# The end of the last feed-forward: when GpSimd leaves, where the squares are summed, and how residual and store are cut

## The chip, the core and the metric

The kernel runs on one core of one Trainium2 chip. A core has TensorE (matrix products, PE in the profile), VectorE (DVE), ScalarE (ACT), GpSimd (POOL) and SyncE (SP), which here only issues DMAs. They run side by side and meet through semaphores. The metric is the device time of one execution in microseconds, the median of several runs; lower is better.

## The reference

Eight stages, each added to the running x of 1024 tokens (16 x 64) by 256 columns: four times an attention-like stage and a feed-forward, each behind a layernorm and a tanh gate. The change concerns the end of the last one.

```python
def _L3_ffn_ref(x, w_gate_up, w_proj):
    ...
    def rms_norm(x):
        eps = jnp.finfo(x.dtype).eps.astype(jnp.float32)
        xf = x.astype(jnp.float32)
        inv = jax.lax.rsqrt(jnp.mean(xf * xf, axis=-1, keepdims=True) + eps)
        return (xf * inv).astype(x.dtype)
    wq_gu = ternary_quant(w_gate_up)
    gu = jnp.einsum('bsd,hd->bsh', x, wq_gu)
    gate, up = jnp.split(gu, 2, axis=-1)
    h = jax.nn.silu(gate) * up
    hn = rms_norm(h)
    wq_p = ternary_quant(w_proj)
    return jnp.einsum('bsh,dh->bsd', hn, wq_p)
...
x = x + jnp.tanh(g_ffn[3]) * _L3_ffn_ref(_layernorm(x, axis=-1), L3_ffn_w_gate_up, L3_ffn_w_proj)
return x
```

h has 1024 columns. The rms norm divides a token's whole row by one number, so the kernel makes the down product from h as it is and multiplies the result by the token's scale.

## The kernel before

The program is written out by hand, engine by engine: one function for each stage and engine, and each engine runs its eight functions in a row (`PE_S`, `ACT_S`, `DVE_S`, `POOL_S`, and `SYNC` for the DMAs). Nothing schedules; the order on an engine is that of the code, and semaphores alone order the engines. x lies in SBUF all along as `xt` (`x_tok` in the profile), eight tiles of 128 tokens by 256 columns.

The last stage is f3. A step n of 16 takes one chunk of 128 of the 1024 hidden columns (`c`) and one half of the tokens (`half`, four tiles of 128). Four steps make a turn, the first turn is written out, the other three are a loop (`f3_loop`). In a step TensorE makes gate and up (line 3490), ScalarE the silu (3512), VectorE the product h (3540) and its square (3542). Since the products are bf16, h and its square are each split in a high and a low part: ScalarE makes `f3hh` and `f3qh` (3516, 3517), VectorE `f3ql` (3529, semaphore `f3_sl`), GpSimd `f3hl` (3567, `f_h_lo` in the profile, semaphore `f3_hl`). `down`, two steps behind, sums the squares over the chunk with a product against ones (3472, one column for each tile, into bank 6 of PSUM) and makes the down product (3475, 256 columns for each tile, into banks 0 to 3), tile by tile, squares and down product of one tile together; it counts up `f3_d`. The last two steps, 14 and 15, have their `down` behind the loop.

When all 16 are counted, VectorE makes the mean square of the eight tiles' tokens (3549), a reciprocal root of it by an integer seed and three Newton rounds (`rsqrt`, lines 161 to 166), the gate's factor (3551), and then for each tile the scaled down product plus x (3553). Through `dve_step` each of the small instructions waits for the one ahead of it.

Every f3 function ends in `finish(e, 9)`: it adds one to `stage_done` (line 146) and waits until the four engines have done so. SyncE waits for the same count, issues one DMA of all of x (3588), and waits for it to land. Behind the functions each engine comes to the end of the block (all recorded at line 84): it drains, reports to GpSimd, and is released by GpSimd when all have reported.

Of the kernel before, what the change touches and what calls it, by code (L numbers as in the profile page):

```python
# [21 lines left out]
ALU = mybir.AluOpType  # L22
# [3 lines left out]
P = 128  # L26
B, S, D = 16, 64, 256
N = B * S
NT = N // P
# [51 lines left out]
def program(nc, a):  # L81

    ctx = ExitStack()
    with ctx:
# [3 lines left out]
        def sem(name):  # L88
            return ctx.enter_context(nc.semaphore(name))


        xt = sb("x_tok", [P, NT, D])
# [8 lines left out]
        onesb = sb("ones_bf16", [P, 2], BF16)  # L101
# [17 lines left out]
        ps = ctx.enter_context(nc.psum_tensor("psum", [P, 8, 512], F32))  # L119
# [3 lines left out]
        dve_step, act_step, pool_step = Chain(sem("dve_step")), Chain(sem("act_step")), Chain(sem("pool_step"))  # L123
# [10 lines left out]
        x_stored = sem("x_stored")  # L134
# [5 lines left out]
        def done(eng, last=None):  # L140

            if last is not None:
                last.then_inc(pe_end, 1)
                n_pe_end[0] += 1
                eng.wait_ge(pe_end, n_pe_end[0])
            eng.sem_inc(stage_done, 1)

        def finish(eng, k, last=None):

            done(eng, last)  # L150
            eng.wait_ge(stage_done, 4 * k)
# [944 lines left out]
        c1_vr = sem("c1_values_ready")  # L1096
        c1_hl = sem("c1_qk_parts_ready")
# [6 lines left out]
        c1_x = sem("c1_x_ready")  # L1104
# [444 lines left out]
        FI = 1024  # L1549
# [1874 lines left out]
        F3_STEPS = 4  # L3424
        F3_TURNS = 2 * FI // P // F3_STEPS
# [3 lines left out]
        f3P = f3TP[:, 4 * FI:6 * FI].rearrange("p (c d) -> p c d", d=D)  # L3429
# [15 lines left out]
        f3_sf = sem("f3_squares_ready")  # L3445
        f3_sl = sem("f3_squares_lo_ready")
        f3_d = sem("f3_down_done")

        def f3_loop(e, body):

# [8 lines left out]
        def f3_pe(e):  # L3459

            turn_pe(e, 4, yt, 8)
            wait_yT(e, 4)
            e.wait_ge(*f3_in.at(64))

            def down(n, c, half, b, first):
                e.wait_ge(f3_hl, n + 1)
                e.wait_ge(f3_sl, n + 1)
                for j in range(4):
                    i = 4 * half + j
                    t = slice(j * P, (j + 1) * P)  # L3470
                    for x, l in enumerate((f3qh, f3ql)):
                        e.matmul(ps[:, 6, i:i + 1], l[:, b, t], onesb[:, 0:1], start=(first and i == 0 and x == 0), stop=False,
                                 skip_group_check=True)
                    for x, l in enumerate((f3hh, f3hl)):
                        ins = e.matmul(ps[:, i // 2, (i % 2) * D:(i % 2 + 1) * D], l[:, b, t], f3P[:, c, :],
                                       start=(first and i % 2 == 0 and x == 0), stop=False, skip_group_check=True)
                ins.then_inc(f3_d, 1)

            def body(it):
                fresh = isinstance(it, int)  # L3480
                for n_ in range(F3_STEPS):
                    n, half = F3_STEPS * it + n_, n_ % 2
                    tk = slice(half * HALF, (half + 1) * HALF)
                    for r, bank, done, ahead, filled in ((0, (4, 7)[n_ % 2], f3_si, 1, f3_g), (1, 5, f3_h, 0, f3_u)):
                        if not fresh or n_ > ahead:
                            e.wait_ge(done, n - ahead)
                        for kc in range(KC):
                            w = f3T[:, r, kc, bass.ds((2 * it + n_ // 2) * P, P)]
                            for x, y in enumerate((yTh, yTl)):
                                ins = e.matmul(ps[:, bank, :], w, y[:, kc, tk], start=(kc == 0 and x == 0), stop=(kc == KC - 1 and x == 1))  # L3490
                        ins.then_inc(filled, 1)
                    if not fresh or n_ > 1:
                        m_ = (n_ - 2) % F3_STEPS
                        c = 2 * it + n_ // 2 - 1
                        down(n - 2, c if fresh else bass.ds(c, 1), half, m_, fresh and n_ < 4)
            f3_loop(e, body)
            for n_ in (2, 3):
                down(F3_STEPS * (F3_TURNS - 1) + n_, FI // P - 1, n_ % 2, n_, False)
            e.wait_ge(f3_d, F3_STEPS * F3_TURNS)
            finish(e, 9)  # L3500

        def f3_act(e):
            turn_act(e, 4, yTh)

            def body(it):
                fresh = isinstance(it, int)
                for n_ in range(F3_STEPS):
                    n = F3_STEPS * it + n_
                    e.wait_ge(f3_g, n + 1)
                    if not fresh:  # L3510
                        e.wait_ge(f3_h, n - F3_STEPS + 1)
                    e.activation(f3g[:, n_, :], ps[:, (4, 7)[n_ % 2], :], ACT.Silu).then_inc(f3_si, 1)
                    e.wait_ge(f3_h, n + 1)
                    if not fresh:
                        e.wait_ge(f3_d, n - F3_STEPS + 1)
                    e.activation(f3hh[:, n_, :], f3h[:, n_, :], ACT.Copy).then_inc(f3_hh, 1)
                    e.activation(f3qh[:, n_, :], f3h[:, n_, :], ACT.Square).then_inc(f3_hh, 1)
            f3_loop(e, body)
            e.wait_ge(f3_hh, 2 * F3_STEPS * F3_TURNS)
            finish(e, 9)  # L3520

        def f3_dve(e):
            ln_tiles(e, NT - 1, NT)
            turn_dve(e, 4, yTh, yTl)

            def squares_lo(n, b):
                e.wait_ge(f3_hh, 2 * n + 2)
                e.wait_ge(f3_sf, n + 1)
                e.tensor_tensor(f3ql[:, b, :], f3sf[:, b % 2, :], f3qh[:, b, :], ALU.subtract).then_inc(f3_sl, 1)

            def body(it):
                fresh = isinstance(it, int)
                for n_ in range(F3_STEPS):
                    n = F3_STEPS * it + n_
                    e.wait_ge(f3_si, n + 1)
                    e.wait_ge(f3_u, n + 1)
                    if not fresh:
                        e.wait_ge(f3_hl, n - F3_STEPS + 1)
                        e.wait_ge(f3_hh, 2 * (n - F3_STEPS) + 2)
                    e.tensor_tensor(f3h[:, n_, :], ps[:, 5, :], f3g[:, n_, :], ALU.mult).then_inc(f3_h, 1)  # L3540
                    e.wait_ge(f3_h, n + 1)
                    e.tensor_tensor(f3sf[:, n_ % 2, :], f3h[:, n_, :], f3h[:, n_, :], ALU.mult).then_inc(f3_sf, 1)
                    if not fresh or n_ > 0:
                        squares_lo(n - 1, (n_ - 1) % F3_STEPS)
            f3_loop(e, body)
            squares_lo(F3_STEPS * F3_TURNS - 1, F3_STEPS - 1)
            e.wait_ge(f3_d, F3_STEPS * F3_TURNS)

            dve_step(e, e.tensor_scalar(f3v[:, :], ps[:, 6, 0:NT], 1.0 / FI, float(np.finfo(np.float32).eps), ALU.mult, ALU.add))
            rsqrt(e, dve_step, f3r[:, :], f3v[:, :], [NT])  # L3550
            dve_step(e, e.tensor_scalar(f3r[:, :], f3r[:, :], gates[:, 7:8], None, ALU.mult))
            for i in range(NT):
                ins = e.scalar_tensor_tensor(xt[:, i, :], ps[:, i // 2, (i % 2) * D:(i % 2 + 1) * D], f3r[:, i:i + 1], xt[:, i, :],
                                             ALU.mult, ALU.add)
            dve_step(e, ins)
            finish(e, 9)

        def f3_pool(e):
            def body(it):
                fresh = isinstance(it, int)  # L3560
                for n_ in range(F3_STEPS):
                    n = F3_STEPS * it + n_
                    e.wait_ge(f3_hh, 2 * n + 1)
                    if not fresh:
                        e.wait_ge(f3_d, n - F3_STEPS + 1)
                    e.wait_ge(f3_hh, 2 * n + 2)
                    e.tensor_tensor(f3hl[:, n_, :], f3h[:, n_, :], f3hh[:, n_, :], ALU.subtract).then_inc(f3_hl, 1)
            f3_loop(e, body)
            e.wait_ge(f3_hl, F3_STEPS * F3_TURNS)
            finish(e, 9)  # L3570


        SYNC = [l0_sync, c1_sync, m1_weights, lambda e: m1_sync(e, a2_ahead, a2_keys_values_ahead), a2_sync, lambda e: m2_sync(e, a3_ahead), a3_sync, f3_sync]
# [8 lines left out]
        @block.sync  # L3582
        def _(e):
            setup_sync(e)
            for stage in SYNC:
                stage(e)
            e.wait_ge(stage_done, 4 * (1 + len(PE_S)))
            e.dma_start(a["out"].rearrange("(t p) d -> p t d", p=P), xt[:, :, :]).then_inc(x_stored, 16)
            e.wait_ge(x_stored, 16)

        @block.tensor
        def _(e):
# [173 lines left out]
```

## Time and profile before

| | |
|---|---|
| median of 3 runs | 1300.43 us (1300.22 to 1301.52) |
| the profiled execution | 1304.3 us |
| its span, first to last instruction | 1302.5 us |
| VectorE's mean square of the last stage starts | 1287.07 us |
| its last residual ends | 1292.98 us |
| store issued, landing | 1293.06 us, 4.4 us later |
| last instruction | 1302.5 us |

Times inside the profile count from the span's start. In a row of the timeline the first number is the start and the second the time taken, both in us; the bracket at the end is the idle time ahead of it and what ended that. In a row by source line come the shortest, median and longest duration in ns, and the first and last start in us. A letter q behind an engine (POOLq) means its sequencer, which handles waits, branches and drains. The three runs and the profiled execution are different executions; the profiled one is 3.9 us longer than the median.

### The profile page before, as it was taken

How to read it: one execution, taken by the hardware profiler on the slowest of the kernel's cores; microseconds unless marked ns; L12 is line 12 of the kernel's file. 1: busy time of each engine (PE TensorE's matmuls, PEld its weight loads, DVE VectorE, ACT ScalarE, POOL GpSimd, SP SyncE). 2: the span in 40 equal slices, each digit the busy share in tenths (PEclk: the TensorE clock that was granted, in tenths of full speed). 3: DMA queues.
4: the chain of work that ended last, by engine and by line, in shares of the span. 5: the costliest groups of instructions: out<-in, count | busy, mean ns of one | idle time of the engine just before them, and what ended most of it. 6: DMA issues, size and time to landing. Idle time of an engine off the chain costs nothing.

```text
span 1302.5 us, 22884 instructions
## 1 busy us (share of the span) xinstructions
PE 1147.4 (88%) x8124; PEld 844.3 (65%) x8147; DVE 850.5 (65%) x1920; ACT 621.5 (48%) x1407; POOL 352.9 (27%) x328
## 2 busy tenths in 40 slices
PE   4867869999969999899999988888998999999894
PEld 3554644444455665889988746666657888898753
DVE  7788966888867663455546585333497777775664
ACT  5575435677733343344433422222266766666252
POOL 0040011222121002222222146566422433334032
PEclk8756976999969999899999889899999999999998
DMA  7010034000032235000000262522371000000100
GB/s 257 2 44 1 1 137 203 1 2 2 2 134 91 88 140 174 1 2 1 1 1 1 92 288 84 196 85 86 101 289 66 17 18 17 17 9 9 49 1 33
DMA packets 44571, 89.30 MB, mean 69 GB/s; under 512 B 7280, under 2 KB 30448, under 8 KB 42672
## 3 DMA queue, kind: packets, MB, share of 16 engines
q1 hardware_dynamic: 39184, 73.45, 15.7%
q0 software_dynamic: 5280, 14.42, 3.4%
q8 instruction: 67, 1.10, 0.4%
q14 instruction: 40, 0.33, 0.1%
HBM read 68.72 MB, written 21.10 MB: 69 GB/s over the span
## 4 chain that ended last, share of the span: by engine, by line
PE 65%; DVE 18%; issue 6%; ACT 5%; DMA 2%; POOL 2%; SPq 1%; another core or an unknown queue 1%; DVEq 0%; ACTq 0%; POOLq 0%; PEldq 0%
PE psum L2566 5%; PE psum L2154 4%; PE psum L3183 4%; PE psum L2126 4%; PE psum L3155 3%; PE psum L2586 3%; PE psum L1702 2%; PE psum L1274 2%; PE psum L3056 2%; PE psum L3103 2%; PE psum L2079 2%; PE psum L3125 2%; PE psum L3490 2%; PE psum L2057 2%; PE psum L1720 2%
## 5 line engine op out<-in xcount | busy, mean ns | idle before, releaser
L1469 DVE TENSOR_REDUCE c_max<-psum 128x2 f32<-128x512 f32 x128 | 84.2, 680 | 19.7 <-PE psum L1274 18.2
L1369 ACT ACTIVATE c_probs<-psum 128x512 f32<-128x512 f32 x128 | 75.1, 597 | 35.6 <-PE psum L1285 35.4
L2566 PE MATMUL psum<-m_experts,m_tileT 128*128 x188 | 69.2, 493 | 19.2 <-issue 13.4
L3183 PE MATMUL psum<-a_wo,a_outT 128*128 128x256 f32 x256 | 75.1, 405 | 0.7 <-DVE x_tok L3365 0.7
L2208 ACT ACTIVATE a_probs<-a_probs,a_max 128x64 f32<-128x64 f32 x128 | 42.7, 334 | 44.9 <-DVE a_max L2264 44.9
L3263 ACT ACTIVATE a_probs<-psum,a_max,a_q_rstd 128x128 f32<-128x128 f32 x128 | 56.8, 458 | 11.3 <-DVE a_max L3313 11.2
L2566 PEld LDWEIGHTS psum<-m_experts,m_tileT 128*128 128x128 f32 x188 | 35.8, 199 | 38.6 <-issue 27.9
L2126 PE MATMUL psum<-ctxT_yT_hi,a_wq 128*128 128x128 f32 x256 | 52.9, 290 | 8.2 <-DVE a_qT L2250 7.1
L2875 POOL DMA_INDIRECT m_back<-m_out_tiles,m_rows_of_slots x47 | 46.8, 995 | 46.9 <-DVE m_out_tiles L2809 39.6
L2643 ACT ACTIVATE m_tile_silu<-psum 128x176 f32<-128x176 f32 x47 | 14.9, 318 | 91.0 <-PE psum L2566 56.3
L2250 DVE TENSOR_TENSOR a_qT<-psum,a_columns 128x512 f32<-128x512 f32 x32 | 22.0, 688 | 55.4 <-PE psum L2126 55.4
L2803 DVE COPY m_tileT<-psum 128x256 f32<-128x256 f32 x47 | 19.9, 424 | 58.6 <-PE psum L2557 30.8
L2190 ACT ACTIVATE a_q_squares<-a_qT 128x512 f32<-128x512 f32 x32 | 20.1, 628 | 77.9 <-DVE a_qT L2250 77.5
L1702 PE MATMUL psum<-m_w,m_tileT 128*128 x120 | 54.5, 597 | 2.8 <-DVE m_tileT L1896 2.2
L3155 PE MATMUL psum<-ctxT_yT_hi,a_wq 128*128 128x128 f32 x256 | 52.1, 286 | 4.9 <-DVE a_q_cos L3324 4.1
L2126 PE MATMUL psum<-ctxT_yT_lo,a_wq 128*128 128x128 f32 x256 | 51.9, 286 | 0.0
L3310 DVE TENSOR_REDUCE a_max<-psum 128x4 f32<-128x512 f32 x32 | 22.1, 690 | 45.2 <-PE psum L3103 45.0
L3155 PE MATMUL psum<-ctxT_yT_lo,a_wq 128*128 128x128 f32 x256 | 51.3, 283 | 0.0
L1274 PE MATMUL psum<-c_qk_stacked 32*128 32x256 bf16 x256 | 50.1, 288 | 1.2 <-ACT c_qk_stacked L1357 0.9
L2869 POOL DMA_INDIRECT y_tok<-m_y,m_tokens x47 | 45.5, 967 | 15.3 <-issue 13.4
L2586 PE MATMUL psum<-m_experts,m_tile_hT 128*128 x188 | 49.5, 387 | 0.0
L2126 PEld LDWEIGHTS psum<-ctxT_yT_hi,a_wq 128*128 128x128 f32 x256 | 42.1, 200 | 10.1 <-DVE a_qT L2250 7.8
(576 smaller groups left out, 3397.6 us busy)
## 6 DMA issues: line engine op xcount, KB each, us to landing
m_w<-m_w SPq DMA_DIRECT2D x8, 1536.0 KB, 14.5
m_experts<-m_e SPq DMA_DIRECT2D x16, 608.0 KB, 12.2
a_wq<-a_wq SPq DMA_DIRECT2D x2, 2048.0 KB
m_rows_back<-m_back SPq DMA_DIRECT2D x4, 1024.0 KB, 8.9
a_ctx_kv<-a_ctx_k_v SPq DMA_DIRECT2D x8, 512.0 KB, 4.3
ctxT_yT_hi<-f_gate_up SPq DMA_DIRECT2D x2, 1024.0 KB
a_v<-a_ctx_kv SPq DMA_DIRECT2D x16, 128.0 KB, 2.7
a_wo<-a_wo SPq DMA_DIRECT2D x1, 2048.0 KB, 7.8
```

Source lines behind the costliest of these rows:

```text
L1274: ins = e.matmul(ps[:, c1_score_bank(n), qt * T1:(qt + 1) * T1], c1QK[r, u % 3, 0, qt * P:(qt + 1) * P], c1QK[r, u % 3, 1, :], start=True, ...
L1369: e.activation(c1P[:, n % 8, :, :], ps[:, 2 + n % 2, :].rearrange("p (k t) -> p k t", k=2), ACT.Exp, scale=float(1.0 / np.sqrt(np.float32( ...
L1469: e.tensor_reduce(c1M[:, u % 2, j, :], ps[:, c1_score_bank(n), :].rearrange("p (q t) -> p q t", q=2), AX.X, ALU.max).then_inc(c1_mx, 1)
L1702: ins = e.matmul(ps[:, 1 + 2 * r + t % 2, :], m1xT[:, t % 2, kc, :], m1w[:, bass.ds(own + (2 * r + kc) * 512, 512)], start=(kc == 0), stop ...
L2126: ins = e.matmul(out[:, :, h, :], a2wq[:, kk, (4 * j + h) * HD:(4 * j + h + 1) * HD], a2tok[kk][:, 1, i * P:(i + 1) * P], start=(kk == 0), ...
L2154: ins = e.matmul(ps[:, 7, 0:D], a2at[:, i % 2, h, :, :], a2wo[h // 8][:, h % 8, :], start=(h == 0 and g is None), stop=(h == HQ - 1), skip ...
L2566: ins = e.matmul(ps[:, 4 + t % 2, 0:M2_UP], m2xT[:, t % 2, kc, :], m2e[:, bass.ds(own + kc * M2_UP, M2_UP)], start=(kc == 0), stop=(kc == ...
L2586: ins = e.matmul(ps[:, t % 2, 0:D], m2hT[:, t % 2, c, :], m2e[:, bass.ds(own + KC * M2_UP + c * D, D)], start=(c == 0), stop=(c == 1))
L2875: e.indirect_dma_start(a["m2_back"], bass.IndirectOffsetOnAxis(m2di[:, t:t + 1], 0), m2out[:, t % M2_BUFS, :], None).then_inc(m2_sc[t % M2 ...
L3155: ins = e.matmul(out[:, :, h, :], a3wq[:, kk, (4 * j + h) * HD:(4 * j + h + 1) * HD], a3tok[kk][:, 1, i * P:(i + 1) * P], start=(kk == 0), ...
L3183: ins = e.matmul(ps[:, 7, 0:D], a3at[:, i % 2, h, :, :], a3wo[:, h, :], start=(h == 0 and g is None), stop=(h == HQ - 1), skip_group_check ...
L3263: ins = e.activation(a3sc[:, u % 3, p_ * P:(p_ + 1) * P], ps[:, u % 2, p_ * P:(p_ + 1) * P], ACT.Exp, bias=a3mx[:, u % 3, p_:p_ + 1], scal ...
```

## The change

Four things. `finish` becomes `done` in all four f3 functions: an engine still counts up `stage_done`, but doesn't wait for the others. The last two steps' products go through a new function, `last_down`: all eight products of the squares first, with an increment of `f3_sums`, then the eight down products, with an increment of `f3_two` behind every second tile; the waits for the low parts of the squares and of h stand apart. VectorE waits for `f3_sums` ahead of the mean square, and for `f3_two` ahead of every second residual; each residual counts up `f3_out`. SyncE issues four DMAs of two tiles each, one behind every second `f3_out`, and waits for `stage_done` and all four landings. The three names are semaphores of an earlier stage, used again.

```diff
--- before.py
+++ after.py
@@ -3445,6 +3445,7 @@
         f3_sf = sem("f3_squares_ready")
         f3_sl = sem("f3_squares_lo_ready")
         f3_d = sem("f3_down_done")
+        f3_sums, f3_two, f3_out = Turn(c1_vr, NT), Turn(c1_hl, 2 * NT), Turn(c1_x, NT)
 
         def f3_loop(e, body):
 
@@ -3461,6 +3462,23 @@
             turn_pe(e, 4, yt, 8)
             wait_yT(e, 4)
             e.wait_ge(*f3_in.at(64))
+
+            def last_down(n, c, half, b):
+                e.wait_ge(f3_sl, n + 1)
+                for j in range(4):
+                    for l in (f3qh, f3ql):
+                        ins = e.matmul(ps[:, 6, 4 * half + j:4 * half + j + 1], l[:, b, j * P:(j + 1) * P], onesb[:, 0:1], start=False, stop=False,
+                                       skip_group_check=True)
+                ins.then_inc(f3_sums.sem, 1)
+                e.wait_ge(f3_hl, n + 1)
+                for j in range(4):
+                    i = 4 * half + j
+                    for l in (f3hh, f3hl):
+                        ins = e.matmul(ps[:, i // 2, (i % 2) * D:(i % 2 + 1) * D], l[:, b, j * P:(j + 1) * P], f3P[:, c, :],
+                                       start=False, stop=False, skip_group_check=True)
+                    if j % 2:
+                        ins.then_inc(f3_two.sem, 1)
+                e.sem_inc(f3_d, 1)
 
             def down(n, c, half, b, first):
                 e.wait_ge(f3_hl, n + 1)
@@ -3495,9 +3513,9 @@
                         down(n - 2, c if fresh else bass.ds(c, 1), half, m_, fresh and n_ < 4)
             f3_loop(e, body)
             for n_ in (2, 3):
-                down(F3_STEPS * (F3_TURNS - 1) + n_, FI // P - 1, n_ % 2, n_, False)
+                last_down(F3_STEPS * (F3_TURNS - 1) + n_, FI // P - 1, n_ % 2, n_)
             e.wait_ge(f3_d, F3_STEPS * F3_TURNS)
-            finish(e, 9)
+            done(e)
 
         def f3_act(e):
             turn_act(e, 4, yTh)
@@ -3517,7 +3535,7 @@
                     e.activation(f3qh[:, n_, :], f3h[:, n_, :], ACT.Square).then_inc(f3_hh, 1)
             f3_loop(e, body)
             e.wait_ge(f3_hh, 2 * F3_STEPS * F3_TURNS)
-            finish(e, 9)
+            done(e)
 
         def f3_dve(e):
             ln_tiles(e, NT - 1, NT)
@@ -3544,16 +3562,18 @@
                         squares_lo(n - 1, (n_ - 1) % F3_STEPS)
             f3_loop(e, body)
             squares_lo(F3_STEPS * F3_TURNS - 1, F3_STEPS - 1)
-            e.wait_ge(f3_d, F3_STEPS * F3_TURNS)
+            e.wait_ge(*f3_sums.at(2))
 
             dve_step(e, e.tensor_scalar(f3v[:, :], ps[:, 6, 0:NT], 1.0 / FI, float(np.finfo(np.float32).eps), ALU.mult, ALU.add))
             rsqrt(e, dve_step, f3r[:, :], f3v[:, :], [NT])
             dve_step(e, e.tensor_scalar(f3r[:, :], f3r[:, :], gates[:, 7:8], None, ALU.mult))
             for i in range(NT):
-                ins = e.scalar_tensor_tensor(xt[:, i, :], ps[:, i // 2, (i % 2) * D:(i % 2 + 1) * D], f3r[:, i:i + 1], xt[:, i, :],
-                                             ALU.mult, ALU.add)
-            dve_step(e, ins)
-            finish(e, 9)
+                if i % 2 == 0:
+                    e.wait_ge(*f3_two.at(i // 2 + 1))
+                e.scalar_tensor_tensor(xt[:, i, :], ps[:, i // 2, (i % 2) * D:(i % 2 + 1) * D], f3r[:, i:i + 1], xt[:, i, :],
+                                       ALU.mult, ALU.add).then_inc(f3_out.sem, 1)
+            e.wait_ge(*f3_out.at(NT))
+            done(e)
 
         def f3_pool(e):
             def body(it):
@@ -3567,7 +3587,7 @@
                     e.tensor_tensor(f3hl[:, n_, :], f3h[:, n_, :], f3hh[:, n_, :], ALU.subtract).then_inc(f3_hl, 1)
             f3_loop(e, body)
             e.wait_ge(f3_hl, F3_STEPS * F3_TURNS)
-            finish(e, 9)
+            done(e)
 
 
         SYNC = [l0_sync, c1_sync, m1_weights, lambda e: m1_sync(e, a2_ahead, a2_keys_values_ahead), a2_sync, lambda e: m2_sync(e, a3_ahead), a3_sync, f3_sync]
@@ -3584,9 +3604,12 @@
             setup_sync(e)
             for stage in SYNC:
                 stage(e)
+            out = a["out"].rearrange("(t p) d -> p t d", p=P)
+            for two in range(NT // 2):
+                e.wait_ge(*f3_out.at(2 * two + 2))
+                e.dma_start(out[:, 2 * two:2 * two + 2, :], xt[:, 2 * two:2 * two + 2, :]).then_inc(x_stored, 16)
             e.wait_ge(stage_done, 4 * (1 + len(PE_S)))
-            e.dma_start(a["out"].rearrange("(t p) d -> p t d", p=P), xt[:, :, :]).then_inc(x_stored, 16)
-            e.wait_ge(x_stored, 16)
+            e.wait_ge(x_stored, 16 * (NT // 2))
 
         @block.tensor
         def _(e):
```

Instructions as they stand in the program. TensorE, the step 14 and what follows the loop, before (step 15 is alike, and its `f_h_squares` and `f_h` parts are those of that step):

```order
L3472 MATMUL psum<-ones_bf,f_h_squares_hi 128x1 [waits f3_squares_lo_ready,f3_h_lo_ready]
L3472 MATMUL psum<-ones_bf,f_h_squares_lo 128x1
L3475 MATMUL psum<-f_wT_projT,f_h_hi 128x256
L3475 MATMUL psum<-f_wT_projT,f_h_lo 128x256
L3472 MATMUL psum<-ones_bf,f_h_squares_hi 128x1
L3472 MATMUL psum<-ones_bf,f_h_squares_lo 128x1
```

and now, from the last two products of squares of step 14 to the first of step 15:

```order
L3470 MATMUL psum<-ones_bf,f_h_squares_hi 128x1
L3470 MATMUL psum<-ones_bf,f_h_squares_lo 128x1
L3477 MATMUL psum<-f_wT_projT,f_h_hi 128x256 [waits f3_h_lo_ready]
L3477 MATMUL psum<-f_wT_projT,f_h_lo 128x256
L3477 MATMUL psum<-f_wT_projT,f_h_hi 128x256
L3477 MATMUL psum<-f_wT_projT,f_h_lo 128x256
L3477 MATMUL psum<-f_wT_projT,f_h_hi 128x256
L3477 MATMUL psum<-f_wT_projT,f_h_lo 128x256
L3477 MATMUL psum<-f_wT_projT,f_h_hi 128x256
L3477 MATMUL psum<-f_wT_projT,f_h_lo 128x256
L3470 MATMUL psum<-ones_bf,f_h_squares_hi 128x1 [waits f3_squares_lo_ready]
```

The products of squares of a step, which stood two by two among the down products, stand together ahead of them, and the wait for GpSimd's `f_h_lo` stands behind them.

VectorE, its last rows, with the order before as - and now as + (`c1_qk_parts_ready` is `f3_two`, `c1_x_ready` is `f3_out`):

```order
-L3551 TENSOR_SCALAR f_scale_of_token<-f_scale_of_token,gates 128x8 [waits dve_step]
-L3553 SCALAR_TENSOR_TENSOR x_tok<-psum,f_scale_of_token,x_tok 128x256 [waits dve_step]
-L3553 SCALAR_TENSOR_TENSOR x_tok<-psum,f_scale_of_token,x_tok 128x256 x7
-L84 UNCONDITIONAL_BRANCH [waits dve_step,stage_done]
+L3569 TENSOR_SCALAR f_scale_of_token<-f_scale_of_token,gates 128x8 [waits dve_step]
+L3573 SCALAR_TENSOR_TENSOR x_tok<-psum,f_scale_of_token,x_tok 128x256 [waits c1_qk_parts_ready,dve_step]
+L3573 SCALAR_TENSOR_TENSOR x_tok<-psum,f_scale_of_token,x_tok 128x256
+L3573 SCALAR_TENSOR_TENSOR x_tok<-psum,f_scale_of_token,x_tok 128x256 [waits c1_qk_parts_ready]
```

The instructions are the same; every second residual now carries a wait of its own. On the queues of SyncE the end of the program is, before and then now:

```order
L3457 DMA f_wT_projT<-f_prepared 128x6144 [waits stage_done]
L3588 DMA out<-x_tok 128x8x256 [waits stage_done]
L84 UNCONDITIONAL_BRANCH [waits x_stored]
```

```order
L3458 DMA f_wT_projT<-f_prepared 128x6144 [waits stage_done]
L3610 DMA out<-x_tok 128x2x256 [waits c1_x_ready] x4
L84 UNCONDITIONAL_BRANCH [waits x_stored,stage_done]
```

The wait for the barrier moved from the store to the end; and on GpSimd the last row, ahead of the drain, was `L84 UNCONDITIONAL_BRANCH [waits f3_h_lo_ready,stage_done]` and is the same without `stage_done`.

## Rows read from the trace of the kernel before

**Rows 1.** The page: its first line and the chain that ended last, by engine.

```profile
span 1302.5 us, 22884 instructions
...
PE 65%; DVE 18%; issue 6%; ACT 5%; DMA 2%; POOL 2%; SPq 1%; another core or an unknown queue 1%; DVEq 0%; ACTq 0%; POOLq 0%; PEldq 0%
```

**Rows 2.** Line 84, the block's end: ns min/median/max, first and last start.

```profile
L84 POOLq EVENT_SEMAPHORE  x2: 17/17/17, 1302.3 to 1302.4; - x2
...
L84 POOLq DRAIN  x1: 9059/9059/9059, 1293.2 to 1293.2; - x1
L84 ACTq DRAIN  x1: 8/8/8, 1293.2 to 1293.2; - x1
L84 DVEq DRAIN  x1: 17/17/17, 1293.3 to 1293.3; - x1
...
L84 SPq DRAIN  x1: 7/7/7, 1297.7 to 1297.7; - x1
...
L84 PEldq EVENT_SEMAPHORE  x1: 51/51/51, 1302.5 to 1302.5; - x1
```

**Rows 3.** Line 146 from 1283 us on: the last stage's increments of stage_done.

```profile
L146 POOLq EVENT_SEMAPHORE  x1: 17/17/17, 1285.8 to 1285.8; - x1
...
L146 DVEq EVENT_SEMAPHORE  x1: 21/21/21, 1293.0 to 1293.0; - x1
```

**Rows 4.** Timeline from 1280 us: GpSimd's last two operations and VectorE's.

```profile
1281.34 1.16 POOL L3567 TENSOR_TENSOR f_h_lo<-f_h,f_h_hi 128x512 bf16<-128x512 f32 x1 [1.53 <-ACT f_h_squares_hi L3517]
1284.04 1.68 POOL L3567 TENSOR_TENSOR f_h_lo<-f_h,f_h_hi 128x512 bf16<-128x512 f32 x1 [1.55 <-ACT f_h_squares_hi L3517]
...
1283.43 1.28 DVE L3529 TENSOR_TENSOR f_h_squares_lo<-f_h_squares,f_h_squares_hi 128x512 bf16<-128x512 f32 x2
...
1287.07 0.17 DVE L3549 TENSOR_SCALAR f_mean_square<-psum 128x8 f32<-128x8 f32 x1 [2.35 <-PE psum L3475]
...
1287.68 0.17 DVE L164 TENSOR_TENSOR newton_a<-f_scale_of_token 128x8 f32<-128x8 f32 x1
...
1289.75 3.23 DVE L3553 SCALAR_TENSOR_TENSOR x_tok<-psum,f_scale_of_token,x_tok 128x256 f32<-128x256 f32 x8
```

**Rows 5.** Timeline of TensorE: steps 14 (from 1284.25) and 15 (from 1285.78).

```profile
1284.25 0.16 PE L3472 MATMUL psum<-ones_bf,f_h_squares_hi 128*128 128x1 bf16 x1 [1.18 <-DVE f_h_squares_lo L3529]
...
1284.28 0.16 PE L3472 MATMUL psum<-ones_bf,f_h_squares_lo 128*128 128x1 bf16 x1
...
1284.30 0.27 PE L3475 MATMUL psum<-f_wT_projT,f_h_hi 128*128 128x256 bf16 x1
...
1284.41 0.27 PE L3475 MATMUL psum<-f_wT_projT,f_h_lo 128*128 128x256 bf16 x1
...
1285.78 0.18 PE L3472 MATMUL psum<-ones_bf,f_h_squares_hi 128*128 128x1 bf16 x1 [0.29 <-POOL f_h_lo L3567]
...
1286.76 0.27 PE L3475 MATMUL psum<-f_wT_projT,f_h_lo 128*128 128x256 bf16 x1
```

**Rows 6.** By source line: the store's issue (ns, start) and landing; those of `a_v`.

```profile
L3588 SPq DMA_DIRECT2D out<-x_tok x1: 395/395/395, 1293.1 to 1293.1; - x1
...
DMA to landing us min/median/max: 4.4/4.4/4.4
...
L3015 SPq DMA_DIRECT2D a_v<-a_ctx_kv x16: 444/590/1704, 968.7 to 1189.2; - x16
...
DMA to landing us min/median/max: 2.5/2.7/3.9
```

**Rows 7.** A stretch of the store: length, five engines idle, clock, DMA share, GB/s.

```profile
1293.90:1297.20 3.30, 0.00 (x0) 0.00 (x0) 0.00 (x0) 0.00 (x0) 0.00 (x0) 0.50 0.94 318
```

**Rows 8.** DMA issues of the whole run: another store, size of one, us to landing.

```profile
a_trig<-ctxT_yT_lo SPq DMA_DIRECT2D x2, 512.0 KB, 2.6
```

**Rows 9.** The program's start, before the first stage: GpSimd's drain.

```profile
L3748 POOLq DRAIN  x1: 188/188/188, 0.3 to 0.3; - x1
```

## The prediction

> **What bounds the kernel now.** I read the end of the run backwards, since every edit lies there. The page's chain of waits gives the span, 1302.5 us, and shows that over the whole run TensorE carries most of it [rows 1]; none of that work is touched. Then the instructions of the block's end, line 84 [rows 2]. There each engine drains, reports, and is released. Four engines drain in 7 to 17 ns. GpSimd's drain takes 9.06 us: it starts at 1293.2, ends at 1302.26, and all that follows it is the release, the last row of which stands at 1302.5. SyncE had drained at 1297.7. So the run ends on GpSimd's drain, and SyncE, with the store behind it, has 4.6 us of slack.
>
> What starts the drain is in the increments of `stage_done` at line 146 [rows 3]: GpSimd gave its own at 1285.8 and had nothing left to do; VectorE gave its at 1293.0, and GpSimd, held in `finish`, drained 0.2 us later. VectorE in turn: it waits 2.35 us for TensorE's last down products, runs thirteen dependent instructions on 8 columns from 1287.07 to 1289.75 (2.68 us), then eight residual instructions in 3.23 us [rows 4]. TensorE's last step started at 1285.78, released by GpSimd's `f_h_lo`, which had taken 1.68 us beside a VectorE operation, where it takes 1.16 us otherwise [rows 4, 5]. Last, the store: issued at 1293.06, landed 4.4 us later [rows 6].
>
> **The change, part by part.** All times are of the profiled execution, whose own time is 1304.3 us, 3.9 us above the median of 1300.43 us; I take the saving in its span off the median.
>
> *GpSimd leaves.* Its drain now hangs on its own last increment. The lag of 0.2 us from the increment at 1293.0 to the drain at 1293.2 stays: 1285.8 + 0.2 = 1286.0. If the drain keeps its 9.06 us it ends at 1295.1, and with the 0.2 us of release (1302.26 to 1302.5) the span would be **1295.3 us by the GpSimd path**, 7.2 us less. ScalarE and TensorE leave early as well; their drains of 8 ns bind nobody.
>
> *The squares first.* For steps 14 and 15 TensorE now runs eight products of one column, then eight of 256. The row that prices them: a pair of one-column products starts 0.03 us apart, the big ones 0.11 us apart [rows 5]. No row shows eight small ones in a row. Low bound: 0.03 each. High bound: the 0.11 of a big one, since each loads as much weight. From 1284.25: low 8 x 0.03 + 8 x 0.11 + 7 x 0.03 = 1.33, so the last square starts at 1285.58, ends 0.16 later at 1285.74, and VectorE follows 0.04 us on (as 1287.07 follows 1286.76 + 0.27), at 1285.8. High: 23 x 0.11 = 2.53, start 1286.78, VectorE at 1287.0. I take 1285.8, the same instruction pair, 1.3 us earlier. The waits hold nothing up on this path: step 15's low squares are complete at 1283.43 + 1.28 = 1284.71. What GpSimd delivers late (1285.73) gates only the big products, which then end near 1286.8, before VectorE needs them.
>
> *Residual by two tiles.* The chain of 2.68 us now starts at 1285.8 and ends at 1288.5; the four waits on pairs of tiles are met 1.7 us before, so they cost at most the attaching to an instruction, which already bears one. Eight instructions in 3.23 us: 1291.7. Behind VectorE's waits nothing else is queued on it. The increment on each instead of on the last I cost at nothing; if it cost something it would have the 0.5 us of slack found below as cover.
>
> *Four stores in place of one.* The first three issue after pairs end, 0.8 us apart, beside VectorE's work. One issue takes 0.40 us on SyncE's queue, and at worst 1.70 us, in the rows of `a_v` [rows 6]. The last goes out 0.08 us behind the last residual (as 1293.06 behind 1289.75 + 3.23): 1291.8. Its landing isn't in the trace. Of the 4.4 us, 3.3 us at 318 GB/s move the megabyte [rows 7], 1.1 us are ahead and behind; a quarter would take 0.8 + 1.1 = 1.9 us (low). High is the undivided 4.4. The nearest store row, `a_trig` with half a megabyte, shows 2.6 us [rows 8], loads of `a_v` 2.5 to 3.9 us. I take 2.6: landed at 1294.4. Then 0.2 us to SyncE's drain (1293.06 + 4.4 = 1297.5 to 1297.7) and 0.2 us of release: **1294.8 us by the SyncE path**, 1294.1 at the low ends.
>
> *High ends of the SyncE path.* Slow squares and a landing of 4.4: 1287.0 + 5.91 + 0.08 + 4.4 + 0.4 = 1297.8. Issues of 1.70 us each, the first at 1288.5 + 0.9 = 1289.4: the last begins at 1294.5, with 3.9 us of landing and 0.4 it is 1298.8. That one I rate unlikely, as the store's own issue row is 0.40.
>
> **The sum.** The span ends with the later path: 1295.3 (GpSimd), 0.5 us behind SyncE's. Saving 1302.5 - 1295.3 = 7.2 us, median 1300.43 - 7.2 = **1293.2 us**, in a profile 1297.1. The parts don't add up singly. The early leave alone would end on SyncE at 1297.7 + 0.2 = 1297.9, 4.6 us saved. Squares and stores alone would leave the drain behind VectorE: 1291.7 + 0.2 + 9.06 + 0.2 = 1301.2, 1.3 us saved. Each removes the other's bound.
>
> **Rules set against the rows.** The rows show a drain of 9.06 us on GpSimd and 7 to 17 ns elsewhere. The Trainium skill, page "VectorE: DVE Perf Modes", section "The DRAIN you can't avoid", holds the drains around a kernel for a constant of about 12 ns on all five engines. By that, GpSimd's row would be waiting and not work, which is the first rival; a 12 ns drain would itself be worth nothing to move. The trace agrees for four engines only.
>
> **Rivals.**
>
> 1. *The drain waits for something that ends later.* It takes 0.19 us at the program's start [rows 9], so its length isn't fixed; at the end it closes 1302.26 - 1297.5 = 4.8 us behind the store's landing. If it is tied to that, it ends at 1294.4 + 4.8 = 1299.2, span 1299.4, saving 3.1: 1297.3 us; with a landing of 4.4, 1299.1. Against it: the store is SyncE's, and nothing is recorded in those 4.8 us that could hold GpSimd. Chance 0.12.
>
> 2. *The drain is shorter where no profile is taken.* The timed runs are 3.9 us below the profiled one. Were all of that the drain (5.2 us), the kernel before would end at 1293.2 + 5.2 + 0.2 = 1298.6 and the new one on SyncE at 1294.8: saving 3.8, 1296.6 us. Shorter than 4.5 us, SyncE ends both, 1297.9 to 1294.8, saving 3.1: 1297.3 us. For it: nothing in the profile says where the 3.9 us lie. Chance 0.12.
>
> 3. *The drain blocks VectorE, and the time gets longer.* Now the drain runs beside VectorE's 5.9 us. The trace shows these two engines disturbing each other: 1.68 against 1.16 us [rows 4]. If the drain held VectorE from the first Newton instruction with two SBUF inputs (1285.8 + 0.6) until it ends at 1295.1, the rest of VectorE's work (1287.68 to 1292.98, 5.3 us) ends at 1300.4, and 0.08 + 2.6 + 0.4 makes the span 1303.5: 1.0 us longer, 1301.4 us; with a landing of 4.4, 1303.2 us. It decides once VectorE is held for more than 1302.5 - 1294.8 = 7.7 us. Against it: the 0.52 us that GpSimd lost are about the length of VectorE's operation (0.68 us), and there VectorE was not the one that lost. Chance 0.04. The page "SBUF — State Buffer" of the Trainium skill, section "SBUF: two separate sides", calls the pair of ports that the two engines share an exclusive lock which blocks the other for the whole instruction; the row agrees for an elementwise GpSimd operation, and no row shows it for a drain.
>
> 4. *The store or the squares at their high ends*, with the drain as forecast: 1297.8 gives 1295.7 us, 1298.8 gives 1296.7 us. It is part of the main case's range.
>
> **How the numbers follow.** Forecast 0.70, with its own range 1292.6 to 1296.0: the GpSimd path is a floor in the span, the median of three differs by some 0.5 us, the top is the SyncE path's high end. Rivals 0.12, 0.12, 0.04; 0.02 for the rest. The range for 8 in 10 reaches over the middles of rivals 1 and 2: 1292.4 to 1297.5 us. A measurement of this kernel can tell about 0.2%, 2.6 us, from no change. The forecast and nearly all of rivals 1 and 2 save over 2.6 us: faster 0.90; their long landings and half of rival 3 lie within it: 0.07; slower 0.03.
>
> **What would show it.** In the profile after: GpSimd's drain starts at 1286.0 and takes 9.06 us; a release at 1295.2, behind SyncE's drain near 1294.6; VectorE's mean square at 1285.8 with small products 0.03 us apart; its last residual at 1291.7; four issues 0.8 us apart and the last landing 2.6 us behind its issue. Rival 1: the drain starts at 1286.0 but is some 13 us long. Rival 2: the profile is as forecast, the medians differ by about half of it. Rival 3: a gap of microseconds ahead of a Newton instruction. I am wrong outright if the drain grows by what it starts earlier.

## The result and the profile after

The changed kernel takes 1292.13 us (median of 6 runs, 1288.04 to 1295.83), the kernel before beside it 1300.57 us (6 runs, 1297.01 to 1301.52): a ratio of 0.9937, 95% interval 0.9913 to 0.9961, or 8.4 us less. Forecast were 1293.2 us and a range of 1292.4 to 1297.5 us; the measured time lies 0.3 us below that range. The direction and the mechanism came as forecast, and the width of the range did not.

The profiled execution took 1291.01 us, with a span of 1289.2 us. Its end reads like this. First the block's end, line 84, which answers [rows 2]; the columns are durations in ns and starts in us.

```profile
L84 POOLq EVENT_SEMAPHORE  x2: 17/17/17, 1289.0 to 1289.1; - x2
...
L84 POOLq DRAIN  x1: 9057/9057/9057, 1279.9 to 1279.9; - x1
L84 PEldq DRAIN  x1: 773/773/773, 1280.2 to 1280.2; - x1
...
L84 SPq DRAIN  x1: 7/7/7, 1288.0 to 1288.0; - x1
...
L84 PEldq EVENT_SEMAPHORE  x1: 51/51/51, 1289.2 to 1289.2; - x1
```

GpSimd still ends the run, but its drain now starts 5.9 us ahead of VectorE's and overlaps VectorE's last work. It took 9.06 us, as before. SyncE drains 1.0 us ahead of GpSimd's release (1288.0 and 1289.0), where it had 4.6 us of slack (1297.7 and 1302.3). GpSimd's own increment of `stage_done`, which answers [rows 3], is 0.1 us ahead of its drain:

```profile
L146 POOLq EVENT_SEMAPHORE  x1: 17/17/17, 1279.8 to 1279.8; - x1
```

The timeline of VectorE, for [rows 4] (start, duration, both in us): the last product h, the mean square, the first of the small instructions, the residuals.

```profile
1276.17 0.69 DVE L3558 TENSOR_TENSOR f_h<-psum,f_silu 128x512 f32<-128x512 f32 x1 [0.69 <-ACT f_silu L3530]
...
1279.71 0.17 DVE L3567 TENSOR_SCALAR f_mean_square<-psum 128x8 f32<-128x8 f32 x1 [0.92 <-PE psum L3470]
1279.91 0.17 DVE L161 TENSOR_SCALAR newton_int<-f_mean_square 128x8 int32<-128x8 int32 x1
...
1282.39 3.23 DVE L3573 SCALAR_TENSOR_TENSOR x_tok<-psum,f_scale_of_token,x_tok 128x256 f32<-128x256 f32 x8
```

VectorE's wait for TensorE fell from 2.35 to 0.92 us. From the mean square on nothing changed: 2.68 us to the first residual and 3.23 us for the eight, with four waits and eight increments more. TensorE, for [rows 5], the first and last squares and the product that waits for GpSimd:

```profile
1278.25 0.18 PE L3470 MATMUL psum<-ones_bf,f_h_squares_hi 128*128 128x1 bf16 x1 [1.10 <-DVE f_h_squares_lo L3547]
1278.29 0.16 PE L3470 MATMUL psum<-ones_bf,f_h_squares_lo 128*128 128x1 bf16 x1
1278.31 0.16 PE L3470 MATMUL psum<-ones_bf,f_h_squares_hi 128*128 128x1 bf16 x1
...
1279.51 0.16 PE L3470 MATMUL psum<-ones_bf,f_h_squares_lo 128*128 128x1 bf16 x1
1279.86 0.28 PE L3477 MATMUL psum<-f_wT_projT,f_h_hi 128*128 128x256 bf16 x1 [0.19 <-POOL f_h_lo L3587]
```

Eight small products in a row keep the 0.03 us from start to start. And the stores, for [rows 6] (issue in ns, first and last start, landing of the four in us):

```profile
L3610 SPq DMA_DIRECT2D out<-x_tok x4: 372/380/395, 1283.3 to 1285.6; - x4
...
DMA to landing us min/median/max: 2.2/2.2/2.2
```

**A measure that leaves the rest of the program out.** The edits act only behind the start of VectorE's last h (step 15). I call the time from there to the end of the span the tail. Before it is 1302.5 - 1282.1 = 20.4 us, after 1289.2 - 1276.2 = 13.0 us: **7.4 us less**. The other 5.9 us by which the two profiled spans differ (13.3 us in all) lie ahead of any changed instruction.

### The profile page after: what moved, and what is told of

Same layout as the page of the kernel before. It is cut to its first block, busy times and chain, and to the rows that moved or that the text cites. A ratio compares the mean times of both kernels' runs of the same rounds, so it can differ in the third digit from the quotient of the medians.

```text
span 1289.2 us, 22885 instructions
## 1 busy us (share of the span) xinstructions
PE 1137.8 (88%) x8124; PEld 838.4 (65%) x8147; DVE 849.7 (66%) x1920; ACT 620.4 (48%) x1407; POOL 352.1 (27%) x328
## 3 DMA queue, kind: packets, MB, share of 16 engines
q1 hardware_dynamic: 39232, 73.45, 15.8%
## 4 chain that ended last, share of the span: by engine, by line
PE 66%; DVE 18%; issue 6%; ACT 5%; DMA 2%; POOL 1%; another core or an unknown queue 1%; SPq 0%; DVEq 0%; ACTq 0%; POOLq 0%; PEldq 0%
PE psum L2154 4%; PE psum L3183 4%; PE psum L2566 4%; PE psum L3155 4%; PE psum L2126 4%; PE psum L2586 3%; PE psum L1702 2%; PE psum L1274 2%; PE psum L3056 2%; PE psum L3103 2%; PE psum L2079 2%; PE psum L3125 2%; PE psum L3145 2%; PE psum L3508 2%; PE psum L2057 2%
```

## The experiments

The tails of all runs, read from the start of the last h and the end of the span; the ratio is to the kernel before on the same chip.

| run | last h, us | end, us | tail, us | median and runs | ratio, 95% interval |
|---|---|---|---|---|---|
| before | 1282.1 | 1302.5 | 20.4 | | |
| after | 1276.2 | 1289.2 | 13.0 | 1292.13 (6) | 0.9937, 0.9913 to 0.9961 |
| after_again | 1282.7 | 1295.7 | 13.0 | 1289.69 (9) | 0.9947, 0.9925 to 0.9968 |
| leave_only | 1277.0 | 1292.8 | 15.8 | 1295.36 (12) | 0.9979, 0.9955 to 1.0003 |
| gpsimd_stays | 1272.3 | 1291.3 | 19.0 | 1295.84 (12) | 0.9994, 0.9974 to 1.0014 |
| both_and_earlier_leave | 1276.7 | 1288.4 | 11.7 | 1290.99 (12) | 0.9945, 0.9923 to 0.9966 |
| one_store | 1248.6 | 1262.9 | 14.4 | 1264.74 (1) | |
| before_drain_ahead | 1251.4 | 1267.2 | 15.8 | 1269.36 (12) | 0.9975, 0.9958 to 0.9992 |
| best_drain_ahead | 1248.3 | 1260.1 | 11.8 | 1264.53 (7) | 0.9945, 0.9924 to 0.9966 |
| after_third | 1252.6 | 1265.6 | 13.0 | 1267.38 (12) | 0.9948, 0.9931 to 0.9966 |

The kernel before had a median of 1297.30 us (32 runs, 1292.48 to 1302.59) beside the runs from after_again to both_and_earlier_leave, and 1272.88 us (23 runs, 1269.46 to 1276.91) on another chip beside the last three; one_store, a single execution, ran on that chip too.

**after_again: is the rest scatter?** No edit.

> The changed kernel once more, unedited. Measured: the tail, from the start of VectorE's last f_h (step 15) to the end of the span; 20.4 us in the profile before, 13.0 us in the one after. Theory (the end is worth its sum, the rest is scatter of the body): tail 13.0 us again, GpSimd's drain 9.06 us; the body ahead of it differs by some us between executions of one and the same kernel, so the median lands anywhere from 1290 to 1295 us and the saving against the kernel before near 7.4 us. Rival (the change speeds up something ahead of the tail too): a saving of 8.4 us or more again, and a body that is shorter than before's by over 1 us in the median of all runs.

The tail was 13.0 us again, every event in it at the same distance from the last h within 0.02 us. Everything ahead of it took 1282.7 us where the first profile has 1276.2: 6.5 us apart, one and the same program. The third stage (`c1`) holds 4.8 us of that. The rows of that stage in the two profiles (stretch, length, then busy time of TensorE, its weight loads, VectorE, ScalarE and GpSimd, the granted clock as a share of 2.4 GHz, DMA share and GB/s), first the first one:

```profile
182.80:355.20 172.40, 158.99 (x1564) 76.12 (x1564) 138.03 (x320) 114.67 (x224) 41.24 (x65) 0.94 0.16 65
```

```profile
182.20:359.40 177.20, 165.57 (x1564) 78.93 (x1564) 138.08 (x320) 114.98 (x224) 41.31 (x65) 0.90 0.16 64
```

The same 1564 products, the same VectorE time, but a granted clock of 0.90 in place of 0.94: more of the stage at the 1.2 GHz level. Over the 32 executions of the kernel before, time and mean granted clock have a correlation of -0.92. The saving by the median was 7.6 us here, by the ratio 6.9 us. So the 8.4 us of the first comparison are 7.4 us of tail and scatter; no speed-up ahead of the tail is needed to explain them, and one of up to about 2 us is not excluded.

**leave_only: one edit alone.** On the kernel before:

```diff
-            finish(e, 9)
+            done(e)
```

in the four f3 functions.

> Kernel before, only the four engines leave without the last barrier; squares, residual and the single store as before. Theory (two paths race, GpSimd's drain and SyncE's store): GpSimd's drain starts 0.2 us after its own last increment and takes 9.06 us, SyncE ends last with its single store: tail 1297.9 - 1282.1 = 15.8 us, 4.6 us less than before. Rival (the drain waits for the store's landing): the drain grows to over 11.5 us and ends 4.8 us behind the landing, tail about 20.4 us, nothing saved.

```profile
L84 POOLq EVENT_SEMAPHORE  x2: 17/17/17, 1292.6 to 1292.7; - x2
...
L84 POOLq DRAIN  x1: 9057/9057/9057, 1280.7 to 1280.7; - x1
...
L84 SPq DRAIN  x1: 7/7/7, 1292.6 to 1292.6; - x1
```

Tail 15.8 us, as the theory has it. GpSimd's drain ended at 1289.8, 2.6 us ahead of the store's landing (SyncE's branch at 1292.4). A drain that waits for the landing can't end ahead of it; the first rival is out. The run now ends on SyncE: its drain and GpSimd's release stand both at 1292.6.

**gpsimd_stays: all the rest without that edit.** On the changed kernel:

```diff
         def f3_pool(e):
             ...
             e.wait_ge(f3_hl, F3_STEPS * F3_TURNS)
-            done(e)
+            finish(e, 9)
```

> The changed kernel, but GpSimd waits for the barrier of all four engines before it drains. Theory: the drain of 9.06 us starts 0.2 us behind VectorE's last residual and ends last; of the whole change only the earlier start of the mean square is left, 1.4 us by the two traces (4.98 us from VectorE's last f_h to the mean square before, 3.54 us after); tail 19.0 us; the split store is worth nothing. Rival (the drain waits for the landing): landing is about 2.2 us earlier besides, tail 20.4 - 1.4 - 2.2 = 16.8 us.

```profile
L84 POOLq DRAIN  x1: 9059/9059/9059, 1282.0 to 1282.0; - x1
L84 SPq COMPARE_BRANCH  x1: 37/37/37, 1284.0 to 1284.0; - x1
L84 SPq DRAIN  x1: 7/7/7, 1284.2 to 1284.2; - x1
```

Tail 19.0 us: 1.4 us saved of 7.4, all of it from the mean square's earlier start. The four stores landed, and SyncE then stood for 7 us, from 1284.2 to its release at 1291.2. The edits don't add up: 4.6 us (leave_only) and 1.4 us make 6.0, together they save 7.4. In timed runs neither part alone is distinguishable from no change with certainty (both intervals include 1), while their tails are plain.

**one_store: the split of the store.** On the changed kernel:

```diff
-            for two in range(NT // 2):
-                e.wait_ge(*f3_out.at(2 * two + 2))
-                e.dma_start(out[:, 2 * two:2 * two + 2, :], xt[:, 2 * two:2 * two + 2, :]).then_inc(x_stored, 16)
+            e.wait_ge(*f3_out.at(NT))
+            e.dma_start(out, xt[:, :, :]).then_inc(x_stored, 16)
```

SyncE's last wait counts one landing in place of four.

> The changed kernel with one store of all of x behind the last residual in place of four. Theory: the landing takes 4.4 us in place of 2.2, SyncE ends last: its drain 2.2 us later than in the changed kernel, 1.1 us of that hidden by GpSimd's drain, so the tail is 13.0 + 1.1 = 14.1 us and GpSimd's drain stays at 9.06 us. Rival (the landing binds by itself): 13.0 + 2.2 = 15.2 us.

```profile
L84 POOLq DRAIN  x1: 9057/9057/9057, 1252.3 to 1252.3; - x1
...
L84 SPq DRAIN  x1: 7/7/7, 1262.7 to 1262.7; - x1
```

Tail 14.4 us, 0.3 above the 14.1 expected: in the changed kernel SyncE's drain comes 11.9 us after the last h, here 14.2, which is 2.3 later in place of 2.2, and the 0.2 us of release behind it I had not counted. The rival would have given 15.2. The split is worth 1.35 us (14.38 - 13.03), and GpSimd's drain hides the other 0.9.

**drain_0, drain_1, drain_8: what a drain of GpSimd's costs.** A bare program, with 0, 1 and 8 indirect gathers on GpSimd.

> A bare program: it loads x, stores it as out and computes nothing else; GpSimd sets 128 row numbers and leaves. It measures GpSimd's drain at the block's end in a program without any DMA of GpSimd's. Theory A (the 9.06 us are a fixed cost of ending on GpSimd): about 9.06 us here as well. Theory B (the cost comes with GpSimd's own gathers and scatters): under 0.2 us, as at the program's start, where it was 0.19 us.

> The bare program (loads x, stores it as out, nothing else computed) with one indirect gather of 128 rows on GpSimd, landed before GpSimd leaves. Theory A (fixed cost): 9.06 us. Theory B (cost of having used an indirect DMA at all): 9.06 us here but not without the gather. Theory C (cost by the number of DMAs): a small part of 9.06 us, since the kernel has 110 of them.

> The bare program (loads x, stores it as out, nothing else computed) with eight indirect gathers, each landed before the next. Theory A and B: 9.06 us as with one. Theory C: eight times the part of one gather.

```profile
L85 POOLq DRAIN  x1: 41/41/41, 1.0 to 1.0; - x1
```

```profile
L85 POOLq DRAIN  x1: 133/133/133, 7.0 to 7.0; - x1
L85 SPq COMPARE_BRANCH  x1: 33/33/33, 10.6 to 10.6; - x1
```

```profile
L85 POOLq DRAIN  x1: 713/713/713, 35.8 to 35.8; - x1
```

In the order 0, 1, 8 gathers: 0.04, 0.13, 0.71 us. That is theory C, (713 - 133) / 7 = 83 ns for each indirect DMA. The profile's page of the kernel before lists 47 gathers, 47 scatters and twice 8 more, 110 in all: 133 + 109 x 83 = 9.2 us, measured 9.06. With one gather the drain was over 3.5 us ahead of the store's landing, once more against the first rival. Since each of these DMAs moves 128 rows, the runs don't tell a cost for each DMA from one for each row. GpSimd's elementwise work adds nothing that can be seen: in best_drain_ahead below, 16 `f_h_lo` operations stand between the two drains, and the second takes 0.03 us. I had taken the 9.06 us as given, and none of my cases said where they come from.

**before_drain_ahead: pay it where GpSimd is idle.** On the kernel before, with the last barrier kept:

```diff
         def f3_pool(e):
+            e.drain()
```

> The kernel before with one more instruction: GpSimd drains once at the start of the last stage, where it is idle until the first f_h_hi; it still waits for the last barrier. Theory (a drain costs about 0.08 us for each indirect DMA of GpSimd's since the last drain, 110 here): the early drain takes 9.0 to 9.3 us and ends before GpSimd's first f_h_lo, the last drain is short (0.04 to 0.2 us), and SyncE ends the run: tail from VectorE's last f_h 15.8 us in place of 20.4, as in the run where only the engines leave early. Rival (the 9.06 us belong to the last drain of a long program, whatever went before): early drain short or also 9 us, last drain 9.06 us, tail 20.4 us.

The new drain (line 3559) and, behind it, the one at the end:

```profile
L3559 POOLq DRAIN  x1: 9057/9057/9057, 1199.9 to 1199.9; - x1
```

```profile
L84 POOLq DRAIN  x1: 38/38/38, 1262.5 to 1262.5; - x1
...
L84 SPq DRAIN  x1: 7/7/7, 1267.0 to 1267.0; - x1
```

The 9.06 us moved as a whole to 1199.9, ended at 1208.9, 3 us ahead of GpSimd's first `f_h_lo` at 1211.96, and the last drain fell to 0.04 us. Tail 15.8 us: one instruction gives the 4.6 us that leaving early gives. So a drain pays for the DMAs since the last one, wherever it stands.

**both_and_earlier_leave and best_drain_ahead: past the changed kernel.** Both sum the squares of steps 14 and 15 ahead of both steps' down products; the first also moves step 15's `f_h_lo` to VectorE so that GpSimd leaves a step earlier, the second has the early drain in its place.

```diff
 def f3_dve(e):
     ...
             squares_lo(F3_STEPS * F3_TURNS - 1, F3_STEPS - 1)
+            e.wait_ge(f3_hl, F3_STEPS * F3_TURNS - 1)
+            e.wait_ge(f3_d, F3_STEPS * (F3_TURNS - 1))
+            e.tensor_tensor(f3hl[:, F3_STEPS - 1, :], f3h[:, F3_STEPS - 1, :], f3hh[:, F3_STEPS - 1, :], ALU.subtract).then_inc(f3_hl, 1)
             e.wait_ge(*f3_sums.at(2))
```

is in the first only, with GpSimd's last turn one step shorter; in both:

```diff
+            for n_ in (2, 3):
+                last_squares(F3_STEPS * (F3_TURNS - 1) + n_, n_ % 2, n_)
             for n_ in (2, 3):
                 last_down(F3_STEPS * (F3_TURNS - 1) + n_, FI // P - 1, n_ % 2, n_)
```

> The changed kernel with two more edits: the squares of steps 14 and 15 are both summed ahead of the down products of both steps, and f_h_lo of step 15 is made by VectorE, so that GpSimd leaves after step 14. Theory: the mean square starts right behind VectorE's extra operation, about 2.75 us after the start of the last f_h in place of 3.54; GpSimd's drain ends about 9.9 us after it and no longer bounds; SyncE ends last: tail about 11.2 us against 13.0 of the changed kernel, 1.8 us less, median 1290 to 1292 us. Rival (the drain needs the engines to be quiet, or grows when it starts earlier): drain over 9.06 us, tail 13 us or more.

```profile
L84 POOLq DRAIN  x1: 9057/9057/9057, 1277.3 to 1277.3; - x1
...
L84 SPq DRAIN  x1: 7/7/7, 1288.1 to 1288.1; - x1
```

```profile
1279.22 0.68 DVE L3571 TENSOR_TENSOR f_h_lo<-f_h,f_h_hi 128x512 bf16<-128x512 f32 x1
1279.82 0.15 DVE L3574 TENSOR_SCALAR f_mean_square<-psum 128x8 f32<-128x8 f32 x1
```

Tail 11.7 us in place of the 11.2 expected. GpSimd's drain keeps its length and is out of the way. The mean square started 3.14 us after the last h, not 2.75, and it follows VectorE's own `f_h_lo` without idle time: that extra operation could only start 2.54 us after the last h, and the step from its start to the next is 0.60 us. TensorE would have let it start a little earlier: its squares of step 15 began at 1279.35 and the last of them ended at 1279.70, 3.02 us after the last h. The median of 1290.99 us is no lower than that of after_again, 1289.69: 1.3 us of tail don't show in these timed runs.

> The changed kernel with the same early drain on GpSimd, and the squares of steps 14 and 15 both summed ahead of the down products of both. Theory: the mean square starts 3.05 us after the last f_h (3.54 in the changed kernel), GpSimd's last drain is over long before, and SyncE ends the run 0.5 us earlier than its path in the changed kernel: tail 11.5 to 11.6 us against 13.0. Rival (last drain 9.06 us again): tail 13.0 us.

```profile
L84 POOLq DRAIN  x1: 34/34/34, 1252.0 to 1252.0; - x1
...
L84 SPq DRAIN  x1: 7/7/7, 1259.9 to 1259.9; - x1
```

Tail 11.8 us, 0.2 to 0.3 above the expected, 1.2 below the changed kernel's. The mean square started at 3.07 us as expected. Then its timeline shows a row that none of the others has:

```profile
1251.37 0.17 DVE L3571 TENSOR_SCALAR f_mean_square<-psum 128x8 f32<-128x8 f32 x1 [0.45 <-PE psum L3470]
1251.57 0.39 DVE L161 TENSOR_SCALAR newton_int<-f_mean_square 128x8 int32<-128x8 int32 x1
1251.99 0.17 DVE L162 TENSOR_SCALAR f_scale_of_token<-newton_int 128x8 int32<-128x8 int32 x1
```

```profile
1250.25 1.68 POOL L3592 TENSOR_TENSOR f_h_lo<-f_h,f_h_hi 128x512 bf16<-128x512 f32 x1 [1.55 <-ACT f_h_squares_hi L3539]
```

`newton_int` takes 0.39 us where it takes 0.17 us elsewhere, and ends at 1251.96, just behind GpSimd's `f_h_lo` at 1251.93. These 0.22 us are the excess over the expected tail: SyncE's drain comes 11.88 us after the last h in the changed kernel, less 0.47 us of earlier mean square, plus 0.22, which is 11.63, as measured. I read it as VectorE held until GpSimd was done; that was not tried by itself. TensorE's clock is no rival: its granted clock is 0.56 from 1251.4 to 1255.0 in this run, where the changed kernel has 1.00 over its last products, and VectorE's rows from 1251.99 on keep their 0.17 us all the same. The slower down products lengthen only TensorE's own drain, to 2.48 us, and nobody waits for that.

**after_third: the changed kernel beside them.** No edit.

> The changed kernel a third time, on the chip of these two runs. Tail 13.0 us. If the executions scatter ahead of the tail as in the runs so far, its median against the kernel before on this chip lies between 5 and 9 us lower; the version with the early drain should come out 1.5 us below it, which the scatter may hide.

Tail 13.0 us a third time. Against the kernel before the median is 5.5 us lower, by the ratio 6.6 us. The version with the early drain has the lowest median of this chip, 1264.53 against 1267.38 us, but its ratio interval and that of the changed kernel overlap almost wholly: better by 1.2 us of tail, not shown by the timed runs.

## Why the prediction was right, and where it was wrong

**The bound.** Right. GpSimd's drain ended the run before, and ends it after. leave_only and gpsimd_stays show both halves: 15.8 and 19.0 us of tail, where the forecast for the one edit was 4.6 us less (measured 4.6) and for the rest without it 1.3 us less (measured 1.4).

**GpSimd leaves.** Right in each number on this path: 0.1 to 0.2 us from its increment to the drain, 9.06 us of drain, 0.2 us of release, 7.2 us saved by this path and 7.4 measured. The path starts from GpSimd's increment, 3.7 us after the last h before and 3.6 after (1279.8 - 1276.2). One row beside it was misjudged without harm: I kept TensorE's drain at 8 ns, and it took 773 ns, since it now follows directly on the last down products; it was over by 1281.0.

**The squares.** The low end held, 0.03 us from product to product; the mean square starts 1.4 us earlier by the distance to the last h (4.98 to 3.54 us), forecast 1.3.

**Residual and stores.** The waits and increments cost nothing. The landing was 2.2 us; I took 2.6, the row of a transfer twice as large, where the low bound of 1.9 us worked out from the store's own stretch [rows 7] was nearer. It cost the forecast nothing: SyncE's path has 1.0 us of slack, not 0.5.

**Rival 1** (the drain waits for a landing) fell with the 9.06 us in the profile after, where it asked for some 13, and with leave_only; **rival 3** (the drain blocks VectorE) fell with the profile after: VectorE's rows beside the drain are those of before to 0.01 us. The exclusive lock of the Trainium skill's page "SBUF — State Buffer", section "SBUF: two separate sides", which I had weighed there, does not show beside this drain. The drain of about 12 ns on all engines, from the section "The DRAIN you can't avoid" of the Trainium skill's page "VectorE: DVE Perf Modes", comes near for GpSimd only where no indirect DMA had been issued since its last drain, 0.03 to 0.04 us at the block's end; with 110 the measured 9.06 us decides.

**Rival 2** (a shorter drain without a profile) rested on a misreading. Each timed execution also has a span of its own, and for all of them, of before and of the versions run beside it, time less span is 1.7 to 2.1 us, like the 1304.3 - 1302.5 of the profiled one. And the 3.9 us between the profiled execution and the median lie within what timed executions alone show, up to 5.3 us above their median of 1297.30 us. The rival's saving of 3.1 to 3.8 us lies outside all three comparisons: the ends of their intervals nearest to no change are savings of 5.1, 4.2 and 4.3 us.

**The step that failed** is the range: "the median of three differs by some 0.5 us", and with it the lower end of 1292.4 us as a floor. The GpSimd path is a floor for the tail, not for the execution, whose other 1280 us move by themselves. Three runs within 1.3 us hid that; 32 runs of the same kernel reach from 1292.5 to 1302.6 us with a standard deviation of 2.9 us, and the nine of after_again from 1286.6 to 1297.5. The evidence was on the table: the profiled execution was a fourth one, 3.9 us off, and I gave it to a rival in place of the scatter. With a standard deviation of 3 us a median of six runs has about 1.25 x 3 / sqrt(6) = 1.5 us of its own (a median scatters 1.25 times as much as a mean), the reference of three runs 2.2 us, and both together 2.7 us; the lower end of a range for 8 in 10, 1.3 standard deviations off, belonged near 1293.2 - 1.3 x 2.7 = 1289.7 us. The point was 1.1 us off; with a scatter of 2.7 us that closeness is partly luck. What bears out the sum is the tail, 7.4 us shorter in three profiles, where 7.2 were forecast.

What stays open: whether the body of the changed kernel is faster by a share of the remaining 1 us, which the timed runs can't tell, and what sets the stretches of lower clock in an execution.

## What to carry to other kernels

Look at the last rows of the span: a drain of GpSimd's costs what its indirect DMAs add up to, and it can be paid early, either by letting GpSimd leave or by a drain where it is idle. Where two paths race to the end, cost each edit on its path and take the later one: here two edits worth 4.6 and 1.4 us alone save 7.4 together. And measure an edit of a few us from a landmark next to it, in the profile; the spread of a range comes from all executions there are, the profiled one among them.

## What the runs showed of the hardware

- A drain on GpSimd took 0.04 us with no indirect DMA since the last drain, 0.13 with one, 0.71 with eight, 9.06 with 110: about 83 ns each, for DMAs of 128 rows. It didn't wait for SyncE's stores, and didn't slow VectorE beside it.
- On TensorE, the drain at the block's end took 0.74 to 2.48 us where it followed directly on queued products, ending 0.05 us behind the last of them, and 8 ns where TensorE had waited for them before (before, leave_only).
- A store of 1 MB landed 4.4 us after its issue, each of four quarters 0.8 us apart 2.2 us after its own.
- VectorE's 128x8 integer instruction took 0.39 us in place of 0.17 us in the one run where it met the end of a GpSimd elementwise operation; the cause was not tried by itself.
- Another chip ran the kernel before in 1272.88 us in place of 1297.30 us. In its profiles the sixth stage, with the 94 gathers and scatters of expert tiles, took 204.3 us (from 735.4 to 939.7 in after_third) where it took 231.4 us in the profile after (729.3 to 960.7); the others agree within a few us. The cause is open.
